# First head through DRAM alone, the other heads' rows from the head stage, six feed-forward steps ahead of the first scores

## The reference, cut to what matters

```python
# layer 0 (x is 1 x 2048 x 128 here), attention on the normalised rows
q, k, v = (x @ W + b for each of Wq, Wk, Wv), split in 16 heads of 8
scores = einsum('bhtd,bhsd->bhts', q, k) * 8 ** -0.5
out = softmax(scores) @ v ; out @ Wo + bo
# layer 0, feed-forward, a gate on the same normalised rows
tanh(x @ weight @ aux_weight1 @ aux_weight2 + bias)
# layer 3: q and k turned by rope, causal softmax, then a top-1 mixture of experts
```

## Time and profile before

| | |
|---|---|
| median of three runs | 1891.17 us |
| the profiled execution | 1891.83 us, of which the traced span is 1890.1 us |
| PE, DVE, ACT, POOL busy | 1628.9, 1425.7, 1113.8, 337.4 us |
| mean granted TensorE clock | 0.929 of full speed |
| end of layer 0's projections to the first instruction of `heads0` | 39.4 to 55.9 us |
| `heads0` | 55.9 to some 740 us |
| end of layer 3's last projection copy to the first instruction of `heads3` | 1389.2 to 1401.7 us |
| `heads3` | 1401.7 to 1821 us |

### The profile page before, as it was taken

The page is one execution under the profiler, slowest core; times in us unless marked ns, Lnnn a source line. Parts: engine busy times, 40 slices in busy tenths (PEclk is TensorE's granted clock), DMA queues, the critical chain, the costliest instruction groups (busy, mean ns, idle before and its releaser), DMA issues. The chain is left out here.

```text
span 1890.1 us, 28648 instructions
## 1 busy us (share of the span) xinstructions
PE 1628.9 (86%) x9625; PEld 632.9 (33%) x9625; DVE 1425.7 (75%) x2696; ACT 1113.8 (59%) x2266; POOL 337.4 (18%) x628
## 2 busy tenths in 40 slices
PE   2789999999999996779997798895549999999987
PEld 1422222222222222434444444684222222222246
DVE  5689999999999963675555606565768999999925
ACT  3158888888888884232222243454214777777754
POOL 0101200001000000000000334553012333312133
PEclk8879999999999998799998899998657999999999
DMA  4101211111110011115333259963430111111132
GB/s 124 49 21 48 75 61 52 48 66 63 58 47 30 23 24 31 67 41 121 94 93 126 94 158 307 298 220 83 156 93 28 50 50 50 49 46 56 37 85 71
DMA packets 76117, 155.62 MB, mean 82 GB/s; under 512 B 16312, under 2 KB 33592, under 8 KB 72276
## 3 DMA queue, kind: packets, MB, share of 16 engines
q1 hardware_dynamic: 64250, 125.63, 21.0%
q0 software_dynamic: 11504, 27.62, 4.7%
q10 hardware_dynamic: 218, 0.55, 0.1%
HBM read 103.41 MB, written 48.89 MB: 81 GB/s over the span
## 5 line engine op out<-in xcount | busy, mean ns | idle before, releaser
L880 ACT ACTIVATE heads_probs<-heads_pS 128x512 f32<-128x512 f32 (+3 forms) x1664 | 819.4, 579 | 169.7 <-PE heads_pS L795 167.7
L904 DVE TENSOR_REDUCE heads_run_max<-heads_pM 128x1 f32<-128x1024 f32 x512 | 600.7, 1219 | 28.5 <-PE heads_pM L771 19.6
L811 PE MATMUL heads_pO<-heads_probs,heads_vh 128*32 128x512 f32 (+2 forms) x3328 | 446.0, 583 | 0.8 <-ACT heads_probs L880 0.7
L771 PE MATMUL heads_pM<-heads_ks,heads_qs 56*128 56x512 bf16 (+3 forms) x1040 | 317.6, 380 | 23.2 <-DVE heads_run_max L915 8.5
L795 PE MATMUL heads_pS<-heads_qs,heads_ks 59*128 59x512 bf16 (+3 forms) x1040 | 292.6, 368 | 0.8 <-ACT heads_probs L880 0.8
L915 DVE TENSOR_REDUCE heads_run_max<-heads_pM 128x1 f32<-128x512 f32 x384 | 246.5, 683 | 7.1 <-PE heads_pM L771 7.1
L771 PE MATMUL heads_pM<-heads_k_first,heads_q_first 56*128 56x512 bf16 x624 | 191.0, 383 | 31.6 <-DVE heads_run_max L944 15.3
L795 PE MATMUL heads_pS<-heads_q_first,heads_k_first 59*128 59x512 bf16 x624 | 180.1, 378 | 4.6 <-ACT heads_probs L880 4.6
L795 PEld LDWEIGHTS heads_pS<-heads_qs,heads_ks 59*128 59x128 bf16 x1040 | 76.7, 93 | 267.3 <-ACT heads_probs L880 232.4
L912 DVE CUSTOM_DVE_ANT_0 heads_masked_out<-heads_pM,heads_mask_end 128x128 bf16<-128x128 f32 (+3 forms) x256 | 121.1, 486 | 11.0 <-PE heads_pM L771 8.5
L1431 ACT ACTIVATE top_act_gate<-top_pG 128x512 f32<-128x512 f32 x68 | 40.6, 597 | 136.9 <-PE top_pU L1387 136.9
(11 more groups left out here) (379 smaller groups left out, 1963.8 us busy)
## 6 DMA issues: line engine op xcount, KB each, us to landing
top_weights<-k_comb_dram SPq DMA_DIRECT2D x128, 128.0 KB, 3.0
second_w<-in_L_W_dram SPq DMA_DIRECT2D x12, 1024.0 KB, 11.5
k_hid_slots_dram<-k_zeros SPq DMA_DIRECT2D x8, 1152.0 KB, 4.4
k_h_slots_dram<-second_work SPq DMA_DIRECT2D x48, 192.0 KB, 2.9
second_work<-k_hid_slots_dram SPq DMA_DIRECT2D x48, 192.0 KB, 3.5
heads_qs<-k_parts_dram SPq DMA_DIRECT2D x40, 192.0 KB
heads_ks<-k_parts_dram SPq DMA_DIRECT2D x80, 96.0 KB
k_parts_dram<-proj_part SPq DMA_DIRECT2D x12, 512.0 KB, 4.1
```

Source lines behind the costliest of these rows:

```text
L771: mm = pe.matmul(pM[:, bank_of(c, j, k), 0:w], qs[c % ROUND][rows, i * P:(i + 1) * P], ks[c % ROUND][rows, b * BLK:b * BLK + w], start=Tru ...
L811: mm = pe.matmul(pO[k * 32:k * 32 + VW, o:BLK], vh[c][:, t, at:at + VW], probs[u % 2][:, k * BLK + o:(k + 1) * BLK], start=first_chunk[u] ...
L880: act.activation(probs[u % 2][:, k * BLK + c0 - b * BLK:(k + 1) * BLK], pS[:, slot, 0:c1 - c0], ACT.Exp)\
L904: dve.reduce_max(run_max[:, i, blocks[0][0] // 2:blocks[0][0] // 2 + 1], both.rearrange("p k c -> p (k c)"), AX.X).then_inc(taken, 2)
```

## The change

What is stored and loaded around the two head stages is put in another order; the same numbers are computed.

1. In both projections SP stores only the first head's 8 rows of each part (32 KB), six stores on semaphores `first_stored`. The stage doesn't wait for them to land.
2. POOL waits for the three q stores and issues the 4 loads of the first q stack, in the projection stage.
3. The k stack of the first head is read back from DRAM as well, by 6 DMAs at the start of the head stage: 3 issued by SP (the copy at row 0), 3 by POOL (the copy at row 64), each after the three k stores have landed. The 14 DMAs of 8 rows are gone.
4. The rows of heads 1 to 15 (480 KB a part) are stored by SP in the head stage, behind its three k loads. SP waits until all six have landed (`others_stored`) before it issues the loads of head 1.
5. In layer 0 `full` is gone: ACT writes hi from PSUM with scale and bias, DVE forms `rest` = scale x product - hi, ACT writes mid = `rest` + bias, DVE forms lo = (`rest` + bias) - mid, both on DVE with one SCALAR_TENSOR_TENSOR in place of one TENSOR_TENSOR.
6. `AT_ONCE` goes from 3 to 6: six feed-forward steps ahead of the first fill.
7. In layer 3 a copy of the causal mask goes from DVE to ACT, and DVE waits for it behind its other presets.
8. PE's first fill waits for both groups of loads (`first_loaded`, `first_by_pool`). The part tiles live until the head stages' end.

```diff
@@ head_projections, SP and POOL
-                    if w == 1:
-                        if a == 0:
-                            sp.wait_ge(ones_in, 1)
-                        for dst, src in first_keys(K, parts[1][a], a):
-                            sp.dma_start(dst, src).then_inc(K.first_loaded[bool(rope)], 16)
-                    sp.dma_start(K.parts[w][:, a, :, :], parts[w][a][:, :]).then_inc(stored[w], 16)
-                    if rope and (w, a) == (1, 0):
-                        load_first_queries(sp)
-            for w in range(2):
-                sp.wait_ge(stored[w], 16 * PARTS)
+                    sp.dma_start(K.parts[w][0, a, :, :], parts[w][a][0:HD, :]).then_inc(first_stored[w], 16)
+            sp.wait_ge(ones_in, 1)
...
             pool.memset(K.first_k[HALF // 2:HALF, :], 1.0).then_inc(ones_in, 1)
+            pool.wait_ge(first_stored[0], 16 * PARTS)
+            for dst, src in first_queries(K):
+                pool.dma_start(dst, src).then_inc(K.first_by_pool[bool(rope)], 16)
@@ head_projections, ACT, layer 0
-                    act.activation(full[:, n % 4, :], pq[:, n % 4, :], ACT.Identity, bias=(bias[:, :], bk)[w],
-                                   scale=scale if w == 0 else 1.0).then_inc(taken, 1)
-                if n < N:
+                    act.activation(parts[w][0][:, cols], pq[:, n % 4, :], ACT.Identity, bias=(bias[:, :], bk)[w],
+                                   scale=(scale, 1.0)[w]).then_inc(hi, 1)
+                elif n < N:
                     act.wait_ge(whole, n + 1)
...
-            else:
-                load_first_queries(act)
@@ head_projections, DVE, layer 0
+                        dve.scalar_tensor_tensor(rest[:, n % 4, :], pq[:, n % 4, :], (scale, 1.0)[w], part, ALU.mult,
+                                                 ALU.subtract).then_inc(r1, 1)
...
+                        dve.scalar_tensor_tensor(parts[w][2][:, cols], rest[:, (n - 1) % 4, :], (bias[:, :], bk)[w],
+                                                 parts[w][1][:, cols], ALU.add, ALU.subtract).then_inc(lo, 1)
@@ first_keys: now from DRAM
+def first_keys(K, half):
+
+    for row, end, src in key_loads(K, 0):
+        yield K.first_k[half + row:half + end, :], src
@@ attention_heads, SP
+            sp.wait_ge(K.first_stored[causal][1], 16 * PARTS)
+            for dst, src in first_keys(K, 0):
+                sp.dma_start(dst, src).then_inc(K.first_loaded[causal], 16)
+            for w in range(2):
+                for a in range(PARTS):
+                    sp.dma_start(K.parts[w][1:, a, :, :], K.parts_made[w][a][HD:, :]).then_inc(others_stored, 16)
+            sp.wait_ge(others_stored, 16 * 2 * PARTS)
             sp.wait_ge(ones_set[1], 1)
             for dst, src, sem in load_stacks(0, 1):
                 sp.dma_start(dst, src).then_inc(sem, 16)
@@ attention_heads, POOL and PE
+            pool.wait_ge(K.first_stored[causal][1], 16 * PARTS)
+            for dst, src in first_keys(K, HALF):
+                pool.dma_start(dst, src).then_inc(K.first_by_pool[causal], 16)
...
+                    if (p, c) == (0, 0):
+                        pe.wait_ge(K.first_by_pool[causal], 16 * FIRST_BY_POOL)
...
-            AT_ONCE = 3
+            AT_ONCE = 6
@@ attention_heads, the mask of layer 3: ACT, DVE
+            if causal:
+                act.activation(mask_end[:, BLK - P:BLK], K.neg_above[:, :], ACT.Copy).then_inc(masked_set, 1)
...
-                dve.tensor_copy(mask_end[:, BLK - P:BLK], K.neg_above[:, :]).then_inc(masked_set, 1)
-                dve.wait_ge(masked_set, 2)
             dve.memset(max_parts[:, PARTS:, :], 0.0)
             dve.memset(run_max[:, :, :], LOWEST).then_inc(preset, 1)
+            if causal:
+                dve.wait_ge(masked_set, 2)
```

More of the change, by code:

```diff
@@ L298, in head_projections @@
         scale = float(np.float32(HD) ** np.float32(-0.5))
-        full = S.sb("full", [P, 4, BLK])
+        full = S.sb("full", [P, 4, BLK]) if rope else None
         rest = S.sb("rest", [P, 4, BLK])
-        parts = [[S.sb(f"part{w}{a}", [P, T], BF16) for a in range(PARTS)] for w in range(2)]
+        parts = K.parts_made
         pq = S.ps("pq", [P, 4, BLK])
@@ L318, in head_projections @@
         N = 2 * NB
-        whole = whole if rope else taken
+        whole = whole if rope else r1
         w_qk = (scaled[:, 0, :] if rope else wq, wk)
         w_swapped = (scaled[:, 1, :], rope[1]) if rope else None
-        def load_first_queries(queue):
-            queue.wait_ge(stored[0], 16 * PARTS)
-            for dst, src in first_queries(K, bool(rope)):
-                queue.dma_start(dst, src).then_inc(K.first_loaded[bool(rope)], 16)
         @block.sync
@@ L419, in _ @@
                     act.wait_ge(r1, n)
-                    act.activation(parts[w][1][:, b * BLK:(b + 1) * BLK], rest[:, (n - 1) % 4, :], ACT.Copy)\
-                       .then_inc(mid, 1)
+                    part, left = parts[w][1][:, b * BLK:(b + 1) * BLK], rest[:, (n - 1) % 4, :]
+                    if rope:
+                        act.activation(part, left, ACT.Copy).then_inc(mid, 1)
+                    else:
+                        act.activation(part, left, ACT.Identity, bias=(bias[:, :], bk)[w]).then_inc(mid, 1)
                 if rope and n == ROUTE_AT[1]:
@@ L435, in _ @@
             dve.wait_ge(K.weights_loaded, WEIGHT_LOADS)
+            if not rope:
+                dve.wait_ge(scaled_q, 1)
             if rope:
@@ L458, in _ @@
                         dve.wait_ge(lo, n - 3)
-                    dve.tensor_tensor(rest[:, n % 4, :], full[:, n % 4, :], parts[w][0][:, b * BLK:(b + 1) * BLK],
-                                      ALU.subtract).then_inc(r1, 1)
+                    part = parts[w][0][:, b * BLK:(b + 1) * BLK]
+                    if rope:
+                        dve.tensor_tensor(rest[:, n % 4, :], full[:, n % 4, :], part, ALU.subtract).then_inc(r1, 1)
+                    else:
+                        dve.scalar_tensor_tensor(rest[:, n % 4, :], pq[:, n % 4, :], (scale, 1.0)[w], part, ALU.mult,
+                                                 ALU.subtract).then_inc(r1, 1)
                 if n >= 1:
@@ L490, in first_queries @@
             yield K.first_q[half + row:half + end, :], src
-def first_keys(K, kept, part):
-    n, at = PRODUCTS[part], sum(PRODUCTS[:part]) * HD
-    for half in (0, HALF):
-        for k in range(n):
-            yield K.first_k[half + at + k * HD:half + at + (k + 1) * HD, :], kept[0:HD, :]
+def first_keys(K, half):
+    for row, end, src in key_loads(K, 0):
+        yield K.first_k[half + row:half + end, :], src
 def causal_plan(causal):
@@ L2569, in recurrent_layers @@
             K.first_q, K.first_k = (first3.enter_context(nc.sbuf_tensor(f"heads3_{n}_first", [P, T], BF16)) for n in "qk")
+            K.parts_made = [[first3.enter_context(nc.sbuf_tensor(f"heads3_part{w}{a}", [P, T], BF16)) for a in range(PARTS)]
+                            for w in range(2)]
             with ExitStack() as rotary:
```

26 lines of the change are left out of this document (15 added, 11 removed).

## The result

The changed kernel takes 1878.08 us (median of 6 runs, 1875.00 to 1882.99), the kernel before in the same comparison 1892.99 (1890.57 to 1898.32). The ratio is 0.9922, 95% interval 0.9902 to 0.9942: faster by 0.8%, as forecast in its direction, but by 14.9 us and not by 21.4. The forecast of 1869.8 us is 8 us too low, and the time is just outside the range of 1865 to 1878. The profiled execution took 1877.64 us (span 1875.9), 14.2 less than that of before.

What follows compares the result with a forecast made beforehand. Bound by the two stage changes, where no engine computes for 16.5 and 12.5 us, and all work ahead of each first fill. Layer 0's 15.0 plus layer 3's 6.4 us off 1891.83 give 1870.4, as median 1869.8 us; range 1865 to 1878.

Steps and rivals of the forecast that it cites:

- The projections of layer 0: Layer 0's projection stage: ACT loses one pass per block, the last parts end at 36.0 us, saving 3.4 us.
- The start of `heads0`: Layer 0's stage change: no wait for landings, barrier 1.0 us, start at 37.6 instead of 55.93 us, 18.3 earlier.
- one of the rivals, with a chance of 0.09: Stage change: the barrier still waits for POOL's q loads; layer 0 gains 8, layer 3 gains 6, total 1877 us; chance 0.09.
- The k loads: First head's k loads in layer 0: 4.0 to 9.4 us at 49 to 115 GB/s, landing taken as 45 us.
- the forecast's 45.4: Layer 0's first fill, at 45.4 us behind six feed-forward steps instead of 60.69, 15.3 us earlier.
- Narrow transfers queue up: First head's q and k loads crawl at 49 GB/s: layer 0 gains 7, layer 3 gains 3; in between 1877 us; chance 0.12.
- A smaller term: Layer 0's last small k stores: landed 2.1 us after their issue, at 38.1 us, releasing the k loads.
- Six steps and the maxima behind them: `heads0`: first three steps 4.8 us, next three 3.0; colder clock makes six more maxima cost 0.3 us.
- The clock rival: `heads0`: PE's pause before the first fill lowers the granted clock, 2 to 4 us back, 1873 us; chance 0.10.
- Layer 3: Stage starts at 1390.2 instead of 1401.69 us, fills at 1395.5 instead of 1403.84; gain 6.4 of a possible 8.3 us.
- the new wait for head 1: Layer 3: head 1's loads wait for six large stores landing at 1403.5, so land at 1419.5 us, 3.7 late.
- The sum: Whole kernel: 15.0 from layer 0 plus 6.4 from layer 3, 21.4 us off 1891.83; median 1869.8 us.

Runs made afterwards that it cites:

- e7_q_by_act: Against the changed kernel, ACT instead of POOL issues layer 0's four q loads, behind its last mid; `heads0` starts at 37.48 us, head 0's maxima take 48.5 us.

## Why the prediction missed

- *The projections of layer 0*: forecast 36.0 for the last lo, measured 35.78. Right, the two-product form at 0.74 and 0.68 us.
- *The start of `heads0`*: "Nothing waits for landings any more, so with the barrier's 1.0 us the stage starts at 37.6". Wrong by 5.1 us: the stage's end did wait for a landing, that of POOL's q loads, in a DRAIN of 7.26 us. It was one of the rivals, with a chance of 0.09 and nearly its price (start 45, total 1877), and the runs with SP and ACT as issuers showed it.
- *The k loads*: "4.0 to 9.4 us, landing at 43.3 to 48.7; I take 45, since loads from two queues can hardly be slower than one queue's best". This is the step that failed beneath the other. Where the fill shows their landing, narrow ones took 5.9 to 10.9 us from their issue in layer 0 and 6.2 to 9.1 from the stage's start in layer 3, over all kernels with them; as ready stacks they took 4.1 to 4.6. With the barrier's wait removed and nothing else, the fill was at 49.95 and 52.45, no earlier than 49.87. Only with both put right does the forecast's 45.4 come about: 46.22, 44.86 and 44.06 in the kernels with ready stacks and ACT. The rival "Narrow transfers queue up" (chance 0.12) had this, and its middle case (first fill at 50, layer 3 gains 4, 1877) is the nearest to the measured 49.87, 4.7 and 1878.08. The two rivals are one mechanism here: the barrier's wait is long because the loads are slow. A smaller term was short too: the small k stores, priced at 2.1 us to land, let SP go on 2.8 to 3.0 us after the end of their issue with ready stacks and 4.4 to 5.0 with narrow q loads on ACT's queue.
- *Six steps and the maxima behind them*: 7.8 and 43.1 (43.4 with the 0.3 for the later maxima) forecast, 7.2 and 43.4 measured, the steps 6.8 to 8.5 over all kernels with six. The clock rival was real as a mechanism and did not fire, for the late start and the six steps left no pause. That is luck: with the forecast's start and these loads it would have fired, as it did in `e7_q_by_act`.
- *Layer 3*: the order of events was right, down to the new wait for head 1. Its sizes were short: fill 7.6 us behind the start instead of 5.3, stores landed at 14.7 instead of 13.3, gain 4.7 instead of 6.4. What decides is head 1: 1.4 us of its lateness are the stores', 0.5 its own loads' (16.5 us instead of 16.0), and 0.2 come back from the earlier start.
- *The sum*: of the missing 7.2 us, 4.1 are layer 0's, 1.7 layer 3's, 0.9 lie between and 0.5 behind. The last two have no cause shown; from head 1's first maximum in layer 0 to the start of `heads3` two executions of this same kernel took 1286.3 and 1284.3 us.

The Trainium skill (DMA: Bandwidth & Descriptors, "Why a DMA increments its semaphore by 16 and not by 1") has the rule that the prediction cited: by it a load of 3 x 8 repeated rows runs on three engines, one of 2 x 24 on two, one of 56 plain rows on fourteen. The traces agree: the q loads by ACT used 10.9% of the 16 engines, 1.7 of them, in 38 to 40 us, and POOL's moved 33 to 164 GB/s against up to 355 for plain rows. I cited it as speaking against the change, and then priced the loads by the best slice of the earlier trace rows, where ten such loads run side by side and hide how slow one is.

## What to carry to other kernels

The loads of 8 to 48 rows, most with a repeated source, ran at 33 to 164 GB/s here, plain ones of 56 rows at up to 355: where such a load stands on the path, lay its data out ready in DRAM and load it plainly. Before moving a stage's start, ask what arrives last behind it; a wait that is removed in front of a later one buys nothing, and the pause that it opens ahead of PE's work can cost more in clock than it gave. DMAs issued by POOL near a stage's end are better issued by SP or ACT, whose DRAIN didn't wait for them, but only once they are fast: the narrow ones ran at half POOL's rate there.

## What the hardware showed

- POOL's DRAIN at a stage's end lasted until its own DMAs had landed: 7.15 to 8.10 us in six executions with narrow loads, 3.70 with wider loads, 4.16 and 4.35 with ready stacks. SP's took 0.06 to 0.24 and ACT's 0.23 to 0.25 with DMAs in flight.
- A pause of PE of 1.2 us left the granted clock at 1.00, one of 2.0 us was followed by 0.85 and then 0.50 until 60 us, 8 us and more. Behind pauses of 2.0 to 7.4 us head 0's maxima took 47.3 to 49.1 us, 3.6 to 5.7 more than without one. What lies between 1.2 and 2.0 us was not measured.
- Small stores queued behind narrow loads on one issuer's queue landed more than 8 us after their issue; with the q loads on ACT's queue it was 4.4 to 5.0.
- Four narrow q loads, 0.46 MB: by POOL 94 GB/s (all traffic) at 23% of the engines in 38 to 40 us, their bytes moved 8 us after the first issue; by ACT and SP 49 GB/s at 11 to 12%, and 10 to 11 us.
